# A transformer layer with routed experts on one core: first input load, scratch clears, operand stacks and the last batch's expert weights moved

## The reference

```
q, k1, k2, v = x @ Wq.T, x @ Wk1.T, x @ Wk2.T, x @ Wv.T          # 16 heads of 8
a    = softmax(causal(q k1' / sqrt 8)) - sigmoid(lam) * softmax(causal(q k2' / sqrt 8))
a    = a / max(sum |a|, 1e-6)
x1   = layernorm(x + (a @ v) @ Wo.T)
xn   = layernorm(x1) * gamma + beta
p    = softmax(xn @ router_w.T / 1.5);  top 2 of 8 experts, by p
y    = sum over the two of p_e * (silu(xn @ W1[e]) @ W2[e])         # 128 -> 512 -> 128
out  = layernorm(x1 + y)
```

## Time and profile before

| | us |
|---|---|
| median of 3 runs | 1146.18 |
| lowest, highest of them | 1145.05, 1156.65 |
| the profiled execution's own time | 1139.17 |
| its span in the trace | 1137.3 |
| busy: PE, DVE, ACT, POOL | 908.5, 935.6, 841.1, 846.0 |

### The profile page before, as it was taken

One profiled execution on the slowest core, in us unless ns is written; L12 is line 12 of the kernel. 1 busy time (PEld: TensorE's weight loads), 2 busy tenths in 40 slices (PEclk: granted clock), 3 DMA queues, 4 the chain that ended last, 5 costly groups with the idle time before them and its releaser, 6 DMA issues. The chain is left out here.

```text
span 1137.3 us, 27887 instructions
## 1 busy us (share of the span) xinstructions
PE 908.5 (80%) x8522; PEld 726.7 (64%) x8522; DVE 935.6 (82%) x2425; ACT 841.1 (74%) x2706; POOL 846.0 (74%) x1144
## 2 busy tenths in 40 slices
PE   2487877879889788978889778978889888978681
PEld 1255555657678576766677566767677676768571
DVE  0499998889998899899999899889999899955132
ACT  1499988688887788788888788787888778853130
POOL 3389978788778888698778988798878986781503
PEclk9579788778998899889999899889999799988696
DMA  3703400533246623482237523582237523246562
GB/s 100 177 10 98 108 1 16 140 100 117 84 122 176 182 76 108 132 246 88 75 122 186 174 74 108 156 238 71 77 120 198 154 73 113 87 147 198 172 215 61
DMA packets 117045, 139.38 MB, mean 123 GB/s; under 512 B 11042, under 2 KB 99490, under 8 KB 116898
## 3 DMA queue, kind: packets, MB, share of 16 engines
q1 hardware_dynamic: 112802, 129.21, 38.3%
q0 software_dynamic: 4096, 8.40, 2.6%
HBM read 107.81 MB, written 29.75 MB: 121 GB/s over the span
## 5 line engine op out<-in xcount | busy, mean ns | idle before, releaser
L700 ACT ACTIVATE exps<-scores,neg_max 128x512 f32<-128x512 f32 (+3 forms) x1024 | 542.9, 551 | 102.1 <-DVE neg_max L989 101.1
L989 DVE TENSOR_REDUCE neg_max<-scores 128x1 f32<-128x512 f32 (+3 forms) x896 | 423.4, 524 | 51.3 <-PE scores L1119 49.1
L627 POOL TENSOR_TENSOR exps<-exps 128x512 f32<-128x512 f32 x256 | 326.7, 1276 | 21.4
L623 POOL TENSOR_SCALAR exps<-exps,inv_l,lam_l 128x384 f32<-128x384 f32 (+3 forms) x448 | 272.7, 615 | 87.2 <-DVE inv_l L964 75.6
L1151 PE MATMUL trans<-ident,exps 128*128 128x128 f32 x1280 | 234.6, 313 | 91.3 <-ACT diffT L707 69.3
L1117 PE MATMUL scores<-stack 72*128 72x512 bf16 (+3 forms) x1024 | 272.6, 335 | 16.6 <-DMA stack<-parts_dram 15.6
L1151 PEld LDWEIGHTS trans<-ident,exps 128*128 128x128 f32 x1280 | 158.4, 158 | 155.3 <-issue 95.3
L700 ACT ACTIVATION_READ_ACCUMULATOR exps<-scores,neg_max 128x1 f32 x1024 | 235.8, 230 | 0.0
L999 DVE TENSOR_REDUCE abs_sum<-exps 128x1 f32<-128x512 f32 (+3 forms) x448 | 222.8, 520 | 8.8 <-POOL exps L627 8.8
L707 ACT ACTIVATE diffT<-trans 128x512 f32<-128x512 f32 x320 | 196.4, 614 | 35.1 <-PE trans L1151 34.3
L1119 PE MATMUL scores<-causal_bf,ident_bf 128*128 128x128 bf16 x1024 | 209.0, 237 | 0.0
(11 more groups left out here) (138 smaller groups left out, 921.6 us busy)
## 6 DMA issues: line engine op xcount, KB each, us to landing
w_sb<-w_dram SPq DMA_DIRECT2D x120, 512.0 KB, 3.8
stack<-parts_dram SPq DMA_DIRECT2D x288, 96.0 KB
parts_dram<-parts SPq DMA_DIRECT2D x104, 128.0 KB
xg<-x_sorted_dram SPq DMA_DIRECT2D x24, 256.0 KB, 4.2
y_sorted_dram<-y_sorted SPq DMA_DIRECT2D x24, 256.0 KB, 4.5
x_in<-x_dram SPq DMA_DIRECT2D x8, 256.0 KB, 4.7
x_res<-x_dram SPq DMA_DIRECT2D x8, 256.0 KB, 4.8
o_dram<-y_out SPq DMA_DIRECT2D x8, 256.0 KB, 2.3
```

Of the source, the lines that this page charges most:

```text
L623: nc.gpsimd.tensor_scalar(diff[:, ring, col:col + w], exps[:, ring, 1, col:col + w], inv_l2[:, i:i + 1], lam_l1[:, i:i + 1], ALU.mult, ALU ...
L627: nc.gpsimd.tensor_tensor(diff[:, ring, :], diff[:, ring, :], exps[:, ring, 0, :], ALU.subtract)\
L700: nc.scalar.activation(exps[:, ring, k, col:col + w], scores[:, c % 2, k, col:col + w], ACT.Exp, bias=neg_max[:, c % 2, k, i:i + 1], accum ...
L989: nc.vector.tensor_reduce(neg_max[:, c % 2, k, i:i + many], scores[:, c % 2, k, col:col + many * w].rearrange("p (i w) -> p i w", w=w), AX ...
```

## The change

Six things:

1. SP issues the load of batch 0's `x_in` ahead of the nine weight loads; slot 0 of body -1 no longer loads it.
2. The two clears of `x_sorted` move from the start to slot 4 of body 0.
3. `rest` has two buffers, used in turn, and DVE waits for POOL's work on the projection two before, not on the one before.
4. `parts_out` becomes three signals, one per projection. `stack_part` waits for projection z just ahead of the three DMAs that read it. ACT and POOL wait for their own projection's signal before they overwrite `parts`.
5. For the last batch, the weights of tiles 0 to 12 go to places of their own: 7 in `exps`, 6 in `diffT`. Their loads wait only for the end of the attention's use of these rings. Tiles 13 and 14 keep the old buffers, and their wait now leads back to tiles of batch 6.
6. Still for the last batch, the 15 loads are issued in two blocks: tiles 0 to 4 at the old place of `weights` 0, which is ahead of `y_out` 3 of batch 6 and of `sorted`; tiles 5 to 14 at the old place of `weights` 1, right behind `sorted`.

```diff
+LATE = EXP_RING + DIFF_RING // 2
+LATE_FIRST, LATE_REST = 0, 1
+LATE_COUNT = 5
+CLEAR_SLOT = 4
...
-        rest = sb("rest", [P, T])
+        rest = sb("rest", [P, 2, T])
...
-        parts_out = signal("parts_out", sum(PARTS_STORED), 16)
+        parts_out = [signal(f"parts_out{z}", PARTS_STORED[z], 16) for z in range(3)]
...
+        late_loaded = [ctx.enter_context(nc.semaphore(f"late_loaded{i}")) for i in range(LATE)]
...
+        late_of = [exps[:, i, :, :].rearrange("p k q -> p (k q)") for i in range(EXP_RING)] + \
+            [diffT[:, i:i + 2, :].rearrange("p k q -> p (k q)") for i in range(0, DIFF_RING, 2)]
+
+        def late(n, j):
+            return n == B - 1 and j < LATE
+
+        def weights_of(n, j):
+
+            return late_of[j] if late(n, j) else w12_sb[:, (n * TILES + j) % WEIGHTS_AHEAD, :]
...
+            sp.dma_start(x_in[:, :, :], rows(x, 0)).then_inc(x_loaded.sem, 16)
             for dst, src in ((wq_sb[:, 0, :], wqT), (wq_sb[:, 1, :], wk1T), (wq_sb[:, 2, :], wk2T),
...
+            def load_weights(n, j):
+                i = n * TILES + j
+                if not late(n, j):
+                    m, used = divmod(i - WEIGHTS_AHEAD, TILES)
+                    while late(m, used):
+                        m, used = divmod(m * TILES + used - WEIGHTS_AHEAD, TILES)
+                    sp.wait_ge(expert_psum.sem, expert_psum.after(m, psum_count[("post", "expert", used)]))
+                    loaded = weights_loaded[i % WEIGHTS_AHEAD].sem
+                else:
+
+                    sp.wait_ge(trans_done.sem, trans_done.after(n, SLOTS))
+                    sp.wait_ge(abs_done.sem, abs_done.after(n, REDUCTIONS[SLOTS]))
+                    sp.wait_ge(pv_done.sem, pv_done.after(n, NG * NT))
+                    loaded = late_loaded[j]
+                which = sp.value_load(owner_int[0:1, n % 2, j:j + 1], min_val=0, max_val=E - 1)
+                sp.dma_start(weights_of(n, j), w12[bass.ds(which, 1), :, :].rearrange("o p f -> p (o f)")).then_inc(loaded, 16)
...
+                    if n < B - 1:
+                        load_weights(n, j)
+                    elif j == LATE_FIRST:
+                        for ahead in range(LATE_COUNT):
+                            load_weights(n, ahead)
+                    elif j == LATE_REST:
+                        for ahead in range(LATE_COUNT, TILES):
+                            load_weights(n, ahead)
...
             def stack_part(n, g):
-                sp.wait_ge(parts_out.sem, parts_out.after(n, sum(PARTS_STORED)))
                 sp.wait_ge(score_done.sem, score_done.after(n - 1, 2 * (g + 1) * GROUP))
                 for z in range(3):
+                    sp.wait_ge(parts_out[z].sem, parts_out[z].after(n, PARTS_STORED[z]))
...
-                    if slot == 0 and b + 1 < B:
+                    if slot == 0 and 0 < b + 1 < B:
...
+                    if slot == CLEAR_SLOT and b == 0:
+                        sp.wait_ge(consts_made, CONSTS)
+                        for i in range(2):
+                            sp.dma_start(pools(x_sorted[i]), xg[:, :, :]).then_inc(sorted_cleared, 16)
...
-            sp.wait_ge(consts_made, CONSTS)
-            for i in range(2):
-                sp.dma_start(pools(x_sorted[i]), xg[:, :, :]).then_inc(sorted_cleared, 16)
...
-                            dve.wait_ge(lo_made.sem, lo_made.after(n, z))
-                            nc.vector.scalar_tensor_tensor(out=rest[:, :], in0=bank[:, :],
+                            m, used = divmod(3 * n + z - 2, 3)
+                            dve.wait_ge(lo_made.sem, lo_made.after(m, used + 1))
+                            nc.vector.scalar_tensor_tensor(out=rest[:, (3 * n + z) % 2, :], in0=bank[:, :],
...
+                    if late(n, j):
+                        pe.wait_ge(late_loaded[j], 16)
```

More of the change, by code:

```diff
@@ L526, in parts_part @@
                 for slot, part in enumerate(STORED[:PARTS_STORED[z]]):
-                    sp.dma_start(scratch[z, :, slot, :, :], parts[:, z, part, :]).then_inc(parts_out.sem, 16)
+                    sp.dma_start(scratch[z, :, slot, :, :], parts[:, z, part, :]).then_inc(parts_out[z].sem, 16)
             def stack_part(n, g):
-                sp.wait_ge(parts_out.sem, parts_out.after(n, sum(PARTS_STORED)))
                 sp.wait_ge(score_done.sem, score_done.after(n - 1, 2 * (g + 1) * GROUP))
                 for z in range(3):
+                    sp.wait_ge(parts_out[z].sem, parts_out[z].after(n, PARTS_STORED[z]))
                     for i, window in enumerate(WINDOWS):
@@ L556, in body @@
                         stack_part(b + 1, NG - 1)
-            sp.wait_ge(consts_made, CONSTS)
-            for i in range(2):
-                sp.dma_start(pools(x_sorted[i]), xg[:, :, :]).then_inc(sorted_cleared, 16)
             run(sp, body)
             sp.wait_ge(y_stored.sem, y_stored.after(B - 1, 1))
-            sp.wait_ge(parts_out.sem, parts_out.after(B - 1, sum(PARTS_STORED)))
+            for z in range(3):
+                sp.wait_ge(parts_out[z].sem, parts_out[z].after(B - 1, PARTS_STORED[z]))
             for i in range(2):
@@ L633, in body @@
                             pool.wait_ge(rest_made.sem, rest_made.after(n, z + 1))
-                            pool.wait_ge(parts_out.sem, parts_out.after(n - 1, sum(PARTS_STORED)))
-                            nc.gpsimd.tensor_copy(parts[:, z, 1, :], rest[:, :]).then_inc(mid_made.sem, 1)
+                            pool.wait_ge(parts_out[z].sem, parts_out[z].after(n - 1, PARTS_STORED[z]))
+                            nc.gpsimd.tensor_copy(parts[:, z, 1, :], rest[:, (3 * n + z) % 2, :]).then_inc(mid_made.sem, 1)
                             pool.wait_ge(mid_made.sem, mid_made.after(n, z + 1))
-                            nc.gpsimd.tensor_tensor(parts[:, z, 2, :], rest[:, :], parts[:, z, 1, :],
+                            nc.gpsimd.tensor_tensor(parts[:, z, 2, :], rest[:, (3 * n + z) % 2, :], parts[:, z, 1, :],
                                                     ALU.subtract).then_inc(lo_made.sem, 1)
@@ L717, in body @@
                             act.wait_ge(psum_of(task).sem, psum_of(task).after(n, psum_count[task]))
-                            act.wait_ge(parts_out.sem, parts_out.after(n - 1, sum(PARTS_STORED)))
+                            act.wait_ge(parts_out[z].sem, parts_out[z].after(n - 1, PARTS_STORED[z]))
                             nc.scalar.activation(parts[:, z, 0, :], bank[:, :], ACT.Copy,
@@ L1089, in side_task @@
                     i = n * TILES + j
-                    w = i % WEIGHTS_AHEAD
                     pe.wait_ge(turned.sem, turned.after(n, j // NT + 1))
-                    pe.wait_ge(weights_loaded[w].sem, weights_loaded[w].after(i // WEIGHTS_AHEAD, 1))
+                    if late(n, j):
+                        pe.wait_ge(late_loaded[j], 16)
+                    else:
+                        w = i % WEIGHTS_AHEAD
+                        earlier_late = sum(late(n, x) for x in range(j) if (n * TILES + x) % WEIGHTS_AHEAD == w)
+                        pe.wait_ge(weights_loaded[w].sem, weights_loaded[w].after(i // WEIGHTS_AHEAD - earlier_late, 1))
                     for f in range(NF):
-                        last = nc.tensor.matmul(bank[:, f * P:(f + 1) * P], w12_sb[:, w, f * P:(f + 1) * P], xgT[:, j // NT % 2, j % NT, :],
+                        last = nc.tensor.matmul(bank[:, f * P:(f + 1) * P], weights_of(n, j)[:, f * P:(f + 1) * P], xgT[:, j // NT % 2, j % NT, :],
                                                 start=True, stop=True)
```

15 lines of the change are left out of this document (4 added, 11 removed).

## The result

| | us |
|---|---|
| changed kernel, median of 6 runs | 1134.30 (1128.31 to 1134.95) |
| kernel before, same comparison | 1148.18 (1145.05 to 1156.65) |
| ratio, 95% interval | 0.9865 (0.9829 to 0.9900) |
| the profiled execution: time, span | 1134.95, 1133.1 |

13.9 us less, where 18.9 were forecast; 1134.3 lies in the range of 1118 to 1135, at its upper edge. By the ratio it is faster by 1.35%, or 15.5 us, beyond the 1% that was called telling; the interval runs from 1.0% to 1.7%, which is 11.5 to 19.6 us.

What follows compares the result with a forecast made beforehand. The start was taken as bound by one chain behind `x_in`, the tail by late expert weights, with nothing paid for in the middle. Head 11.4 + tail 7.5 = 18.9 us off the median 1146.18 gave 1127.3, range 1118 to 1135.

Steps and rivals of the forecast that it cites:

- recorded signs of being wrong: First turn over 2 us later against body 8's end, gathers over 0.3 apart, or middle grown by over 3 us.
- x ahead, 9.2: Start: first transposition at 9.3 instead of 18.53 us, 9.2 gained (9.0 to 9.5); weights' delay 0 to 0.5, taken as 0.2.
- the clears' price of 0: Body 0, slot 4: moved clears cost nothing, covered by batch 0's attention; at most 8 us if they delay later stack groups.
- rest and stack, 0.8 + 1.4: Start: two buffers for rest save 0.8 us, stack waits by projection 1.4; together 2.2, bounds 0 and 3.4.
- Head: Start up to first scores: 9.2 + 2.2 = 11.4 us gained, first scores at about 32.0.
- Late weights, 7.5: Tail, edits 5 and 6: 8.3 - 0.8 = 7.5 us gained, with a lower bound of -3.
- 8.3 from full supply of weights: Tail: with weights always there PE ends at 1107.2 instead of 1115.54 us; stalls not of weights stay.
- 0.8 for PE's late start: Tail: bytes ahead of `xg` make PE's first turn 0 to 2 us late, taken as 0.8.
- Rivals 1 and 2: Start: edits 3 and 4 give nothing, 1129.5 us, chance 0.16; tail: DVE and ACT chain holds PE, 1133.8 us, chance 0.13.
- Rival 3: Tail: weight stream slows thirteen indirect DMAs; 1142.5 us at 1.58 more each, 1163.6 at 3.2; chances mild 0.06, strong 0.03.
- lower bound of -3: Tail: if indirect DMAs take only 0.8 us more each, the tail's gain is about -3 to 2.
- estimate with that page's 436 GB/s: Tail: late loads' bytes pass in 8.9 us without holding up `sorted`; the sum would be 0.8 us better.

Runs made afterwards that it cites:

- e4_again: The changed kernel, unchanged, run again for a second trace: 1123.08 us against 1136.25 for the kernel before, ratio 0.9888.
- e2: Edits 5 and 6 alone, with the start as in the kernel before: 1133.47 us against 1136.25 for the kernel before, ratio 0.9967.
- e1_head: The changed kernel without the late weights (edits 1 to 4 only): 1125.89 us against 1136.25 for the kernel before, ratio 0.9919.
- e3_block1: The changed kernel with one load in the first block instead of five: 1119.88 us against 1136.25 for the kernel before, ratio 0.9852.
- e8: The changed kernel with only the two clears back at the start: 1132.32 us, one execution, beside one of the kernel before at 1155.35.

## Why the prediction was right, and where it was off

- **What bounds the kernel.** Right: the start hung on `x_in` behind the clears and on the chain to the stack, the tail on weights. That nothing is paid for in the middle held as far as it was measured: the halves add up to the whole (10.4 + 2.8 = 13.2), and from the first scores to `owner_int` it is 1010.0 us before and 1008.5 in e4_again; a loss of two or three us would not show. Two of the recorded signs of being wrong did appear: a middle over 3 us longer, in the first pair of traces (11.4 us), which e4_again answers, and a first turn over 2 us later, in e4_again and e2 (2.4 and 3.1 us behind `owner_int`), which is the price below.
- **How near it was.** The time is in the range, 0.7 us from its edge, but the gain is below the forecast's own 15 to 21.5 by medians (13.9) and at its low end by the ratio (15.5); the range holds it because the rivals' times were taken in. The absolute time is partly luck: the kernel before took 1148.18 us in this comparison and 1136.25 in another, where the changed one took 1123.08.
- **x ahead, 9.2.** 9.43 at the first transposition, 8.85 at the first scores. The weights' delay (the last one issued at 5.15 instead of 4.56, so 0.59 us) did not show, as in the lower bound: PE's first instruction, the weight load for lam, starts at 7.73 us in both traces. For the clears' price of 0 there is this: no engine waits for a stack read between the first scores and 149 us in the changed kernel's trace.
- **rest and stack, 0.8 + 1.4.** 1.05 and 1.73 singly, 2.11 together. Head: 11.4 forecast, 10.96 in the trace, 10.4 (by the interval, 6.4 to 12.2) in the times.
- **Late weights, 7.5.** This is the term that was mis-sized: 2.8 by medians, by interval 1.9 to 5.7; 3.7 by the ratio, 3.7 to 4.8 in the sums of the table against the trace before. Two steps failed. *8.3 from full supply of weights* came out at 6.4 to 7.2 from the first turn (42.4 to 36.0 and 35.2): the sum has 26.3 us from the second turn to the end of the last expert group, and it is 28.2 and 27.3 in the changed kernel's two traces. Their waits for `hT` add up to 3.3 us (0.66, 0.17, 1.59, 0.28 and 0.61) and 2.65, against the 2.4 left for them; and a wait costs more than its bracket, since PE advances 0.90 us per group of eight when nothing stops it, and the last group in e4_again started 1.66 us behind the one before with 0.61 in its bracket. *0.8 for PE's late start* came out at 1.6 to 3.1. I had counted bytes ahead of `xg` in SP's queue and SP's issue time, and put the scatters in a parenthesis. The runs show that with five loads the scatters' landing holds back the issue of `xg`: 5.20 us from the last one's start in e4_again, 2.24 with a block of one. With nine loads the counted mechanism shows as well, in the 9.07 us from the issue of `xg` to the first turn.
- **How the 4.7 us missing from 7.5 are shared.** With a block of one the tail gives 6.0 us by the medians of the same comparison (1125.89 in e1_head, 1119.88 in e3_block1). So 3.2 are the four extra loads, and 1.5 are left for the first step. By the ratios it is 7.6 for a block of one and 3.7 for five, so the extra loads are nearly all of it; the first step is the less certain of the two.
- **Rivals 1 and 2** are nearer in number than the forecast (16.7 and 12.4 us less, where 13.9 were measured by medians and 15.5 by the ratio), but what they say did not happen: edits 3 and 4 gave 2.11 us at the first scores, and the early weights found their taker, as the third column shows.
- **Rival 3** had the right place and the wrong handle. The indirect DMAs kept their 0.30 us of distance in every kernel; it is their completion that came late. The 1.88 us before one gather, which the rival built on, says nothing of the weight stream: it stands before the second gather of batch 6 in all 13 traces (1.77 to 1.89), whatever is in flight. The lower bound of -3 taken from its mild form does not follow either: 0.8 us each leaves the tail a gain of 2.4, and -3 needs 1.2 each. The gathers of batch 6 too began later, 16.8 us behind `owner_int` against 12.5, and that cost nothing: DVE's waits for gathers are eight and 13.4 us in all from 1054 us on, against eight and 13.5 before, all of batch 7.
- The rule that I took from the Trainium skill, one ring served in order and rings by turns, was applied to SP's ring alone, where it spoke against the loads ahead of `sorted`; for POOL's scatters, in another ring, nothing was drawn from it. The estimate with that page's 436 GB/s, by which `xg` would not be held up, failed: the window of the changed kernel around the first turn, 1066 to 1076 us, has 300 GB/s, and the first turn came 1.6 to 3.1 us later. The same section ("DMA: Bandwidth & Descriptors", "Queues, rings and completion order") also states that the write which raises a completion semaphore lands only after all earlier writes of that DMA engine, across its queues. That rule is the one that bears on the case: it would have a scatter's semaphore wait for weight data issued by SP. The traces agree with it (2.24 us with one load, 4.04 to 5.83 with five in three traces, at most 3.31 in e8); no run separates it from plain sharing of bandwidth.
- The frame of comparison: the prediction was taken from the median, and it was right to do so; the profiled execution had the short distance of the faster comparisons (above), and a forecast of 1120 from it would have been 14 us off.

## What to carry to other kernels

Prefetch by need, not by room: in this kernel a block of loads issued early was paid for by the small DMAs that had to land meanwhile, and one load ahead of the critical read gave 3.2 us more than five. An input that starts the chain goes first in the queue; bulk clears behind it may stay where they are. Before two traces are subtracted, look for stretches in which an engine stops without a releaser, and take several traces before such a stretch is put down to an edit.

## What the runs showed of the hardware that was not expected

- The landing of POOL's indirect writes depends on what SP has in flight: from the start of the last 64 KB scatter to the read that waits for it, 2.24 us with one weight load beside the scatters, and 4.04, 5.20 and 5.83 with five; in a fourth trace with five (e8) at most 3.31.
- SP's time to issue is not fixed: five 512 KB loads took 5.13, 5.54, 7.95 and 8.64 us in four traces (the two longest are those with the stops), and four `xg` reads 2.03 us behind five loads and 4.85 behind nine.
- PE stopped for 6 us among 40 short matmuls with no releaser, in five traces of 13 and at the same place, whatever the kernel, and the distance around it grew from 110.1 to 111.3 us to 118.3 to 119.9. In the same five ACT's last copy of batch 6 came 2.4 to 4.6 us behind the matmuls that it copies, in the other eight 0.03 or 0.04.
